# Another order of the stages inside a pass, on four engines of a software-pipelined tower

## What is computed

```python
# block 1, per sequence
scores  = einsum('d,bijd->bij', attn_scale, tanh(q[:, :, None, :] + k[:, None, :, :]))
attn    = softmax(scores) @ v @ Wo + bo
x       = layer_norm(x + attn, g1, beta1)
h       = layer_norm(x + relu(x @ W1 + bf1) @ W2 + bf2, g2, beta2)
# block 2: h + causal_attention(layernorm(h)), 8 heads of 128
# block 3: t = layernorm(h) * g + b
top2    = top_k(softmax(t @ Wr @ codebook.T / TEMP), 2)
moe     = sum over the two experts of  w * (silu(t @ W1[e] + b1[e]) @ W2[e] + b2[e])
hmoe    = moe + 0.25 * shared(t)
out     = h + hmoe + ffn(layernorm(hmoe))
```

## Time and profile before

| | us |
|---|---|
| median of 3 runs | 834.74 (834.18 to 837.39) |
| the profiled execution | 835.15, its span 833.3 |
| busy in the span: PE, DVE, ACT, POOL | 773.8, 635.4, 625.2, 357.1 |
| tower, first add to the table of tiles | 12.3 to about 597 |

### The profile page before, as it was taken

How to read it: one execution, slowest core, us unless ns; L and a number is a source line. 1 busy time by engine, 2 the same in 40 slices (tenths; PEclk the granted TensorE clock), 3 DMA queues, 4 the chain that set the end, 5 groups by cost and what they waited for, 6 DMA issues and landing times.

```text
span 833.3 us, 21564 instructions
## 1 busy us (share of the span) xinstructions
PE 773.8 (93%) x7301; PEld 599.3 (72%) x7301; DVE 635.4 (76%) x1665; ACT 625.2 (75%) x1455; POOL 357.1 (43%) x464
## 2 busy tenths in 40 slices
PE   2586999999999999999999999998899899999898
PEld 1365576676766766767667667775789899999787
DVE  5899999999999999999999997543433345443685
ACT  3686999998989989989999898664355466665454
POOL 3111133455445464554454534557336455555211
PEclk9889999999999999999999999999799999999999
DMA  3940000000000000000000000000299999995511
GB/s 95 249 93 4 4 7 9 13 11 13 11 17 13 12 18 14 11 15 11 14 13 11 16 11 7 15 16 19 76 318 398 375 393 402 308 360 188 159 32 38
DMA packets 50161, 79.01 MB, mean 95 GB/s; under 512 B 7556, under 2 KB 34267, under 8 KB 50064
## 3 DMA queue, kind: packets, MB, share of 16 engines
q1 hardware_dynamic: 33888, 65.01, 23.1%
q0 software_dynamic: 5664, 7.92, 3.5%
q10 hardware_dynamic: 10512, 4.83, 2.1%
HBM read 63.95 MB, written 15.92 MB: 96 GB/s over the span
## 4 chain that ended last, share of the span: by engine, by line
PE 47%; DVE 30%; issue 10%; DMA 4%; POOL 2%; SPq 2%; ACT 2%; DVEq 0%; POOLq 0%; ACTq 0%
DVE arena L930 15%; PE big L1688 7%; PE b_s L1372 6%; PE big L1484 4%; PE b_o L1526 4%; PE b_qk L1699 3%; DMA arena<-in_wpack 3%; PE b_s L1699 3%; PE big L1744 3%; PE big L1512 2%; DVE mx L1056 2%; PE b_s L1757 2%; PE big L1505 1%; PE b_qk L1757 1%; DVE stat_h L972 1%
## 5 line engine op out<-in xcount | busy, mean ns | idle before, releaser
L930 DVE TENSOR_TENSOR arena<-qT,b_qk 128x2304 f32<-128x2304 f32 x128 | 322.4, 2534 | 0.2
L678 ACT ACTIVATE arena<-arena 128x2304 f32<-128x2304 f32 x128 | 270.0, 2125 | 14.3 <-DVE arena L930 14.2
L1372 PE MATMUL b_s<-arena,apad 128*32 128x192 f32 x3072 | 156.3, 339 | 16.1 <-ACT arena L678 10.5
L837 ACT ACTIVATE act_h<-big,arena 128x128 f32<-128x128 f32 x324 | 92.7, 369 | 71.6 <-PE big L1688 71.6
L1372 PEld LDWEIGHTS b_s<-arena,apad 128*32 128x32 f32 x3072 | 88.9, 112 | 79.3 <-issue 39.2
L646 POOL DMA_INDIRECT eo_dram<-gT,toff x81 | 79.7, 984 | 94.1 <-DVE gT L1257 90.4
L574 POOL TENSOR_TENSOR kept<-kept,rs 96x384 f32<-96x384 f32 x64 | 55.5, 867 | 132.5 <-DVE rs L1062 132.5
L743 ACT ACTIVATE kept<-big,mx 96x96 f32<-96x96 f32 x256 | 82.7, 335 | 20.7 <-DVE mx L1056 20.5
L1688 PE MATMUL big<-hbT,arena 128*128 128x128 f32 x648 | 87.0, 278 | 5.6 <-DMA arena<-in_wpack 4.1
L1688 PEld LDWEIGHTS big<-hbT,arena 128*128 128x128 f32 x648 | 79.6, 193 | 6.6 <-issue 5.6
L1246 DVE TENSOR_SCALAR hbT<-b_t,cols 128x128 f32<-128x128 f32 x81 | 33.2, 410 | 61.9 <-PE b_t L1681 61.9
(11 more groups left out here) (224 smaller groups left out, 1431.9 us busy)
## 6 DMA issues: line engine op xcount, KB each, us to landing
arena<-in_wpack SPq DMA_DIRECT2D x81, 578.0 KB, 9.0
prT<-rows_dram ACTq DMA_DIRECT2D x73, 64.5 KB
rows_dram<-act_h SPq DMA_DIRECT2D x1, 4128.0 KB, 23.4
arena<-eo_dram SPq DMA_DIRECT2D x4, 512.0 KB, 8.0
x_dram<-res SPq DMA_DIRECT2D x16, 96.0 KB, 1.8
out<-of SPq DMA_DIRECT2D x12, 128.0 KB, 1.8
eo_dram<-gT,toff POOLq DMA_INDIRECT x81, 5.5
rows_dram<-rows_now,slots POOLq DMA_INDIRECT x64, 2.3
```

The costliest lines, as they stand in the source:

```text
L678: act.activation(v, v, ACT.Tanh).then_inc(s["tanh"], 1)
L837: last = act.activation(act_h[:, i, c * TILE:(c + 1) * TILE], big[i][:, c * TILE:(c + 1) * TILE], ACT.Silu, bias=wslot[:, slot, 2 * DFF + ...
L930: dve.tensor_tensor(ring[c % TRING].rearrange("p (x m n) -> p x m n", m=CQ, n=N), qv.unsqueeze(3).to_broadcast([D, SPLIT * QG, CQ, N]), kv ...
L1372: last = pe.matmul(b_s[32 * a:32 * a + 32, 0:SPLIT * N], apad[:, 31 - line:63 - line], t[:, :, a, m, :], start=(line == 0), stop=(line == ...
```

## The change

The order of the `at` lines in `body` is changed on POOL, ACT, DVE and PE, `BIG_ORDER` follows PE's new order, and no instruction is added or taken away. `T_ORDER` and `YA_ORDER` stay. Where the point at which a pass begins moves, the k of the stages moves by one with it; apart from that the stages keep their lag between engines, with these exceptions: `x_rows` goes from behind `add 4` to ahead of `add 0`, for the next pair (k from 0 to -1), and `setup` runs earlier, on PE at k = 0 instead of 1, on DVE at k = -1 instead of 1.

More of the change, by code:

```diff
@@ L616, in body @@
             def body(n):
+                at(n, 6, both_hot)
+                at(n, 6, counted)
+                at(n, 6, keep_rows)
+                at(n, 5, roots_h1)
+                at(n, 6, cum_pair)
+                at(n, -1, gather_emb, 0)
+                at(n, 4, normalise, 0)
+                at(n, 6, scatter_rows, 0)
+                at(n, -1, gather_emb, 1)
+                at(n, 3, setup)
+                at(n, 3, root, "x2")
+                at(n, 5, residual)
                 at(n, 0, keep_x)
-                at(n, -1, gather_emb, 0)
+                at(n, 4, normalise, 1)
+                at(n, 3, root, "h0")
+                at(n, 4, normalise, 2)
+                at(n, 6, scatter_rows, 1)
                 at(n, 4, normalise, 3)
                 at(n, 2, root, "x1")
[L621 to L635, removed]
             in_turns(body)
@@ L1144, in body @@
                 at(n, 1, add, 7)
-                at(n, 5, chosen)
+                at(n, 2, x1_norm)
+                at(n, 5, one_hot)
                 at(n, 3, mask_max, 0)
-                at(n, 2, x1_norm)
                 at(n, 0, queries)
-                at(n, 5, one_hot)
+                at(n, -1, x_rows)
                 at(n, 0, add, 0)
+                at(n, 5, ranks)
+                at(n, 4, h1_stats)
                 at(n, 0, add, 1)
+                at(n, 4, means, "h1")
                 at(n, 3, inv_sums, 0)
-                at(n, 4, h1_stats)
                 at(n, 1, softmax1_max)
-                at(n, 4, means, "h1")
+                at_end(n, 6, shared_rows, 0)
                 at(n, 0, add, 2)
+                at_end(n, 6, shared_rows, 1)
                 at(n, 4, variance, "h1")
-                at(n, 5, ranks)
+                at(n, 3, mask_max, 1)
+                at(n, 3, mask_max, 2)
                 at(n, 0, add, 3)
-                at(n, 4, h1_norm)
                 at(n, 2, x2_stats)
                 at(n, 1, p1T_copy)
+                at(n, -1, setup)
                 at(n, 2, means, "x2")
[L1164 to L1170, removed]
+                at(n, 4, h1_norm)
             in_turns(body)
@@ L1586, in body @@
             def body(n):
+                at(n, 3, ffn1, 0)
+                at(n, 2, score, 6)
+                at_end(n, 5, shared1, 1)
+                at(n, 2, score, 7)
                 at(n, 3, ffn1, 1)
-                at(n, 4, heads_v, 1)
[L1589 to L1593, removed]
+                at(n, 4, scores, 1)
+                at(n, 4, scores, 2)
@@ L1594, in body @@
+                at(n, 0, setup)
+                at_end(n, 6, shared2, 0)
+                at(n, 1, score, 0)
+                at(n, 3, ffn2)
+                at(n, 2, p1_turn)
+                at(n, 1, score, 1)
+                at(n, 4, heads_v, 0)
+                at(n, 4, heads_v, 1)
+                at(n, 5, tn_turn)
+                at(n, 4, o_begin)
+                at(n, 2, attend1)
+                at_end(n, 6, shared2, 1)
+                at(n, 4, pr_turn, 0)
                 at(n, 4, heads_v, 2)
-                at(n, 4, o_begin)
@@ L1596, in body @@
-                at(n, 1, setup)
-                at(n, 1, score, 1)
-                at(n, 4, scores, 2)
+                at(n, 4, scores, 3)
                 at(n, 1, score, 2)
-                at_end(n, 6, shared2, 0)
-                at(n, 5, tn_turn)
-                at(n, 2, attend1)
+                at(n, 5, router)
+                at(n, 4, heads_v, 3)
                 at(n, 2, products)
-                at_end(n, 6, shared2, 1)
-                at(n, 4, heads_v, 3)
-                at(n, 4, scores, 3)
@@ L1626, in body @@
-                at(n, 4, pr_turn, 3)
+                at(n, 2, x1_turn)
                 at(n, 4, attend2, 2)
+                at(n, 5, ranks)
+                at(n, 4, attend2, 3)
+                at_end(n, 4, shared1, 0)
                 at(n, 3, heads_g, 3)
[L1629 to L1635, removed]
```

96 lines of the change are left out of this document (48 added, 48 removed), and 8 rows, old and new, of the table BIG_ORDER.

## The result

Runs of the changed kernel have a median of **842.7 us** (841.27 to 843.91), beside 835.9 us for the kernel before on the same chip: a ratio of **1.0088**, with a 95% interval of 1.0069 to 1.0107. The prediction was 841.2 us, slower. The profiled execution of after took 842.24 us, its span 840.4 against 833.3.

The account below looks back on a forecast made before the run. DVE and PE were taken to share the bound of the steady stretch. Start +10.0, nine steady passes +2.4, ramp -2, last passes -1.9, drain -2 gave +6.5 on the median 834.74: 841.2 us, range 832 to 849.

Parts of the forecast that it names:

- The start: Before pair 0, early setup waits for row_fbf at 19.0; first add at 23.75 instead of 12.31, net +10.0 us.
- POOL's chain: Steady pass, variance of h1 to root of x2: 8.44 us; x2_norm free at Q (start of queries) + 18.7, waiting 0.75.
- The port: Steady pass, x2_norm held by POOL's SBUF reads on the shared port: 0.74 us, between 0.3 and 1.5, or nought.
- POOL goes first throughout: Rival: residual and keep_x both pass ahead of x2_norm, or x_rows is held in full; pass 34.0, 847 us, chance 0.23.
- Behind x2_norm: Rest of the steady pass: x2_norm to router 1.8 us, router to qk 10.79, then 1.02 to queries.
- A sign that was ill put: Prediction called wrong if POOL reaches the root of x2 before DVE has finished add 4.
- The gain at qk: Steady pass, qk ahead of score 5 on PE and a longer cover on DVE: up to 0.87 us a pass.
- The first rival: Gain at qk wins, DVE keeps the port for both halves of x2_norm: pass 32.4, 833 us, chance 0.28.
- faster: Rival: the port also costs nothing and PE meets no wait from router to qk; pass 31.9, 829 us, chance 0.07.
- The ramp: Early passes, DVE idle 3.2 us in two passes, at x2_stats for ffn2 and at queries: -2 us (0 to -4).
- The last passes: Passes 14 and 15 have no gathers on POOL, so neither the wait nor the port loss: -1.9 us.
- the drain: End of the tower, scores 1 and 2 come earlier and POOL has no gathers: -2 us (-4 to +1), an estimate.

Follow-up runs that it names:

- e4: Changed kernel with the root of x2 on POOL put ahead of gather_emb 1 instead of behind it: 830.09 us, 0.9939 of the kernel before.
- e3: Changed kernel with residual and keep_x on POOL put behind normalise 1, away from x2_norm: 832.25 us, 0.9968 of the kernel before.
- e12: Order of e5 with score 6 and score 7 put ahead of ffn1 0 on PE: 835.39 us.
- e1: Changed kernel with setup late again on PE and DVE, and x_rows of pair 1 behind it: 833.64 us, 0.9982 of the kernel before.
- e5: Changed kernel with the edits of e1 and e4 together: 821.19 us, 0.9827 of the kernel before.
- e8: Changed kernel with residual alone put behind normalise 1 on POOL, keep_x left behind the root of x2: 836.73 us, 1.0019 of the kernel before.
- e2: Kernel before with setup alone moved ahead, of xs_turn 0 on PE and queries 0 on DVE: 842.76 us, 1.0099 of the kernel before.
- e7: Changed kernel with qk put back behind score 5 on PE: 857.63 us; the profiled run took 881.13 us.

## Why the prediction was right, point by point

- **The start**, +10.0 predicted, +9.5 measured; first add 23.67 for 23.75. The steps hold: `setup` on PE at 19.32, bounded by the landing of `row_fbf`. Two experiments, one from each side, show that it adds in full.
- **POOL's chain.** Predicted: eight instructions in 8.44 us, `x2_norm` at Q + 18.7 and a wait of 0.75. Measured: 8.20 us (303.56 to 311.76), Q + 18.76 (`queries` at 293.13), a wait of 0.46. The chain was shorter and began later, since `x_rows`, held for 0.27 us (0.66, and 0.39 in the kernel before), delays the variance of h1; I had 0.2 for that, but at another place of the sum. DVE itself was later too, so the wait is smaller.
- **The port.** 0.74 predicted, between 0.3 and 1.5; 1.02 measured. This is the term of the pass that was mis-sized: I had the two engines in turn, but the first half, issued at 311.89 during the first `residual`, ended behind the second, and the second half behind `keep_x`. The mechanism is that of the rival "POOL goes first throughout", which put 1.5 us on it and so 34.0 on the pass. It was less because a half that was held ends 0.14 to 0.16 us behind POOL's instruction, not its full 0.34. The Trainium skill, "SBUF — State Buffer", section "Who interferes with whom", says of the ports that DVE and POOL (GpSimd) share that they are an exclusive lock, and that the order of issue decides who blocks. `keep_x` and the second half agree with it (0.81 us instead of 0.34), and so does e4 from the other side. For the first half the trace goes further than the rule: POOL's second instruction in a row went ahead of a DVE instruction that was already waiting. That is not general. `x_rows`, issued at 326.79 while POOL copied its rows (L600), ended 0.27 us behind that copy, and there it was POOL's next copy that took longer, 0.38 us instead of the 0.20 of the kernel before (last line):

```profile
326.57 0.61 POOL L600 COPY rows_now<-tn 96x512 f32<-96x512 f32 x1
327.13 0.38 POOL L602 COPY rows_now<-choice 96x4 f32<-96x4 f32 x1
...
319.21 0.20 POOL L602 COPY rows_now<-choice 96x4 f32<-96x4 f32 x1
```

  What decides which of the two goes first was not tried.
- **Behind x2_norm:** from its start to `router` 2.77 us, less the hold 1.75 (1.8 predicted); `router` to `qk` 10.87 (10.79); `qk` to `queries` 0.92 (1.02). The pass: 33.33 for 33.3. That it came out so close is in part luck: the hold was 0.28 us longer than forecast, POOL's chain 0.24 shorter.
- **A sign that was ill put.** The prediction calls itself wrong if POOL reaches the root of x2 before DVE has finished `add 4`. That happened: the root began at 311.01, and `add 4` ended at 311.43. But `x2_norm` waits for the root's end (311.76), and the prediction's own sum has the root begin at Q + 17.90 (18.72 less 0.10 and 0.72), ahead of DVE's 17.96. The sign contradicted the sum; the other signs came as stated.
- **The gain at qk**, up to 0.87 us a pass: the wait went as predicted, but the value is not the wait's. Alone, in the kernel before, it is nothing. The sum didn't suffer, since it followed the chain and not the saved wait. The first rival fell on the port: it had DVE keep it for both halves, and where nothing held them (e3) its pass of 32.4 and its 833 us came about, 32.44 and 832.25. The pass of 31.9 of the rival "faster", without a wait of PE, is that of e4.
- **The ramp**, -2 predicted (0 to -4), +0.5 measured: the step that failed. The wait for `ffn2` went, and two others came (DVE, 66 to 100 us):

```profile
76.75 0.36 DVE L960 TENSOR_REDUCE nmax<-b_s 128x2 f32<-128x192 f32 x1 [2.15 <-PE b_s L1372]
...
98.44 0.55 DVE L1056 TENSOR_REDUCE mx<-big 96x4 f32<-96x384 f32 x1 [1.38 <-PE big L1505]
```

  `softmax1_max` waits for `score 7`, now behind `ffn1 0`, and `mask_max 0`, straight ahead of `queries`, for `scores 0`. e12 shows that a wait taken away at one place comes at the next. How much each makes is open: with PE's order as in the changed kernel the ramp took 113.7 to 116.5 us in five other profiles (e1, e3, e4, e5, e8), with the order before 114.2 and 115.4 (before and e2), and in its third pass PE's granted clock was anywhere from 0.78 to 0.94. So the 0.5 itself can't be told from nothing; what is shown is that the 2 us didn't come.
- **The last passes** -1.9, measured -2.0; **the drain** -2 (called an estimate), measured -2.8. Kernels with the changed order on PE and DVE show the same (from the last `queries` to the table 112.5 us in the changed kernel, 113.2 in e3 and 113.3 in e4; 116.2 before, and 116.6 in e2, which has the old order). Which of the moved stages makes it was not tried.

In sum +6.5 predicted and +7.1 in the span: the ramp was put 2.5 us too low, the drain 0.8 and the start 0.5 too high, and 0.4 went behind the table. That these nearly cancel is luck as well; the start and the steady passes, on which the forecast rested, came within 0.5 us.

## What to carry to other kernels

Follow a moved stage through the queue that it now stands in, one pass round from queue to queue: here the sum over that loop came out within 0.1 us (two of its terms missed by a quarter of a us each, in opposite directions), while the waits that the order was to remove said little on the time. An instruction that another engine waits for wants to be early in its queue, and behind it something that doesn't touch what the waiting engine needs; a DMA issue of 1 us did both. A one-time setup put ahead of the first pair made the first add wait for its last load, 11.4 us later than before, and nothing behind paid back the 9.5 us that remained at the second pair.

## What the runs showed of the hardware

- POOL's instructions in a row can hold a DVE instruction with two SBUF inputs for more than one of them: 0.88 us instead of 0.34, ending 0.14 us behind the second `residual`. At another place of the same pass DVE came in behind the first (`x_rows`).
- What was held ends a short time behind POOL's instruction, and the longer the more columns it has: 0.03 us for the subtraction with 2 (308.26 behind `keep_x` at 308.23, kernel before), 0.14 to 0.16 for the held halves of `x2_norm` with 128, 0.27 for `x_rows` with 256 (changed kernel).
- Behind a wait of PE the granted clock fell. In the profiled run of e7, PE stood still for 1.79 us at `router`; then the granted clock was 0.50, the lower of its two levels (1.2 GHz), from about 334 to 340, and eight matmuls of `attend2` took 1.91 us instead of 1.04. From `router` to `xa_turn` it took 7.56 us (331.93 to 339.49) instead of 4.77 (314.66 to 319.43) in the changed kernel, whose wait at the same place is 1.33 us and whose clock stays at 1.00. The wait came again in each of the nine steady passes, each 37.5 us long. That the longer wait brings the lower clock is not shown: one of four runs of the same kernel was 23.5 us shorter.
- The experts' stretch, the same in all orders, took from 233.3 to 237.3 us in the profiled runs. Differences of 2 us between single profiles are therefore not read as the order's.
